# Attention and experts of a transformer layer on one core: two instruction blocks joined into one

## What is computed

```
xn  = layernorm(x)
out = x + attention(xn) + experts(xn)

attention: 16 heads of 16, each token sees the 129 tokens within 64 positions; qkv = xn @ Wqkv + bqkv,
           softmax over the band, then @ Wout + bout
experts:   logits = xn @ router_w + router_b, the best 2 of 8 experts, softmax over these two;
           each expert is relu(xn @ w1 + b1) @ w2 + b2 with 1024 hidden numbers
```

## Time and profile before

| | us |
|---|---|
| median of 3 executions | 956.04 |
| the profiled execution | 957.17 |
| its span, from the first to the last instruction | 955.1 |
| barrier between norm_project and attend | about 100 |
| barrier between attend and experts | about 498 |
| mean granted clock of TensorE, share of full | 0.988 |

### The profile page before, as it was taken

The page is one execution under the profiler, slowest core; times in us unless marked ns, Lnnn a source line. Parts: engine busy times, 40 slices in busy tenths (PEclk is TensorE's granted clock), DMA queues, the critical chain, the costliest instruction groups (busy, mean ns, idle before and its releaser), DMA issues. The chain is left out here.

```text
span 955.1 us, 27555 instructions
## 1 busy us (share of the span) xinstructions
PE 903.1 (95%) x7684; PEld 876.4 (92%) x7684; DVE 824.7 (86%) x2171; ACT 740.7 (78%) x1985; POOL 480.5 (50%) x700
## 2 busy tenths in 40 slices
PE   4989799899999999999969999999999999999996
PEld 3878788889999999999969999999999999999996
DVE  5876699998888888888857999999999999999995
ACT  3545699899999999999956777777777776777773
POOL 5120013236465646555544666556666666556663
PEclk9999799999999999999998999999999999999999
DMA  4979532344444444455335222222222222221210
GB/s 143 322 268 308 169 79 75 117 122 136 136 136 135 137 135 133 136 141 148 105 87 163 37 34 44 46 36 36 34 34 43 47 49 49 35 44 35 36 22 1
DMA packets 69867, 95.33 MB, mean 100 GB/s; under 512 B 15549, under 2 KB 48960, under 8 KB 69696
## 3 DMA queue, kind: packets, MB, share of 16 engines
q1 hardware_dynamic: 52800, 77.97, 27.0%
q0 software_dynamic: 17024, 16.88, 11.2%
HBM read 62.91 MB, written 35.53 MB: 103 GB/s over the span
## 5 line engine op out<-in xcount | busy, mean ns | idle before, releaser
L1029 ACT ACTIVATE weights_qkv<-weights_qkv,low 128x256 f32<-128x256 f32 (+1 forms) x512 | 240.2, 480 | 1.1 <-DVE low L832 1.1
L1456 ACT ACTIVATE hid<-ps_experts,b_s 128x256 f32<-128x256 f32 x312 | 131.0, 473 | 117.5 <-PE ps_experts L1523 87.4
L1344 POOL DMA_INDIRECT out<-y,target x78 | 137.3, 1761 | 127.4 <-DVE y L1422 113.8
L843 DVE TENSOR_TENSOR pt<-ps_attend,pt 128x512 fp32r<-128x512 f32 (+1 forms) x256 | 158.4, 620 | 39.9 <-ACT pt L1042 39.3
L1123 PE MATMUL ps_attend<-pt,v_m 128*80 128x256 f32 (+7 forms) x1536 | 187.8, 271 | 2.3 <-DVE inv_t L856 1.8
L1539 PE MATMUL ps_experts<-w_hi,h_hi 128*128 128x256 f32 x624 | 175.4, 281 | 1.1 <-DVE h_lo L1391 1.1
L1523 PE MATMUL ps_experts<-xgt_hi,w_hi 128*128 128x256 f32 x624 | 173.7, 278 | 2.8 <-DVE xgt_lo L1382 2.8
L1123 PEld LDWEIGHTS ps_attend<-pt,v_m 128*80 128x80 f32 (+3 forms) x1536 | 171.4, 162 | 4.2 <-issue 4.2
L1523 PE MATMUL ps_experts<-xgt_hi,w_lo 128*128 128x256 f32 x624 | 173.6, 278 | 0.0
L1523 PE MATMUL ps_experts<-xgt_lo,w_hi 128*128 128x256 f32 x624 | 173.5, 278 | 0.0
L1539 PE MATMUL ps_experts<-w_lo,h_hi 128*128 128x256 f32 x624 | 172.6, 277 | 0.0
(11 more groups left out here) (174 smaller groups left out, 2008.6 us busy)
## 6 DMA issues: line engine op xcount, KB each, us to landing
weights_qkv<-in_w SPq DMA_DIRECT2D x15, 1024.0 KB, 7.1
qk_hi<-weights_qkv SPq DMA_DIRECT2D x16, 512.0 KB, 4.8
qk_lo<-weights_qkv SPq DMA_DIRECT2D x16, 512.0 KB, 5.5
q_st<-qk_hi SPq DMA_DIRECT2D x128, 64.0 KB
k_st<-qk_hi SPq DMA_DIRECT2D x128, 64.0 KB
weights_qkv<-in_x SPq DMA_DIRECT2D x8, 512.0 KB, 4.3
xn_rows<-weights_qkv SPq DMA_DIRECT2D x8, 512.0 KB, 5.2
k_st<-qk_lo SPq DMA_DIRECT2D x64, 64.0 KB
```

Of the source, the lines that this page charges most:

```text
L843: v.tensor_tensor(lo[:, f:l], ps[:, bank_t[h], 0:l - f], hi[:, f:l].bitcast(F32), ALU.subtract).then_inc(s_plo, 1)
L1029: ins = act.activation(wt[:, ring, at_tile(i)], wt[:, ring, at_tile(i)], ACT.Exp, bias=low[:, ring, i:i + 1], scale=-1.0, accum_out=total[ ...
L1344: pool.indirect_dma_start(out_tokens, bass.IndirectOffsetOnAxis(ap=target[:, h:h + 1], axis=0), y[:, h], None, bounds_check=T - 1, oob_is_ ...
L1456: ins = act.activation(hid[:, n % 2, j], ps[:, bank_h[n], j * ROWS:(j + 1) * ROWS], ACT.Relu, bias=b1[:, ds(e * FC + 2 * n + j, 1)])
```

## The change

Attention and experts become one block; the block of norm_project stays. `g.block` is opened once, and both functions add their instructions to it, so each engine goes from its last instruction of attend to its first of experts with no barrier. For that:

- The operands of the experts become views of buffers that attention has finished with: `w1_hi`, `w1_lo` and the rows of ring 1 lie in `q_st`, `w2_hi` in `v_m`, `w2_lo` in `k_st`, `xt_hi`, `xt_lo`, the rows of ring 2 and `h_hi` in `work` (which is `pt` during attention), `h_lo` in `split` (which is `a_hi` and `a_lo`). The same two buffers hold `xt_lo`, `w_lo` and `xt_hi` of norm_project.
- The 65 semaphores of both stages are raised once, by GpSimd in norm_project, and so are the two `s_out`.
- GpSimd fetches the rows of step 0 (`gather_first`) within the last batch, after the bias additions of head 14 and ahead of head 15.
- The preamble of the experts moves into the tail of attend, between its instructions.
- `ident_r` is copied in norm_project and `b1` is loaded in the first batch of attend.

```diff
@@ norm_project, GpSimd; below it VectorE
+                start(pool, g.later.values())
+                start(pool, g.s_out)
                 pool.wait_ge(s_rstd, 1 + START)
                 pool.memset(g.q_st[:].bitcast(F32), 0.0).then_inc(s_zero, 1)
...
+                v.wait_ge(s_ident, 2 + START)
+                v.tensor_copy(g.ident_r[:], g.ident[:])
                 statistics(0, 0)
@@ attend, SyncE
                 def first_batch():
                     next_stack(0, 2)
+                    sp.dma_start(g.b1[:], g.b1_cols).then_inc(s_b1, 16)
                     next_stack(0, 3)
...
-                sp.wait_ge(s_rows, 16 + START)
-                sp.wait_ge(s_wload, 32 * (E - 1) + 16 + START)
@@ attend, GpSimd, in the loop over heads
                             if last:
                                 add_bias(b, 1, n - 14)
+                        if last and n == 14:
+                            gather_first()
@@ attend, VectorE, behind the last batch
+                first = v.value_load(g.step_expert[0:1, 0:1], min_val=0, max_val=E - 1)
...
+                lo_of_w1(0)
                 v.wait_ge(s_pv, HC * 2 * B + START)
                 v.wait_ge(s_invs, 2 * B + START)
...
-                add_projected(B - 1, 0, bank_t[0])
-                add_projected(B - 1, 1, bank_t[1])
+                v.wait_ge(s_xhi, 1 + START)
+                v.tensor_tensor(g.xt_lo..., ps[:, bank_t[0], :], g.xt_hi..., ALU.subtract).then_inc(s_xlo, 1)
+                for h in range(2):
+                    add_projected(B - 1, h, bank_last[h])
+                lo_of_w1(1)
+                half = slice(0, FC // 2)
+                v.wait_ge(s_w2hi, 1 + START)
+                v.tensor_tensor(g.w2_lo[:, half], g.w2_of(first)[:, half], g.w2_hi[:, half].bitcast(F32),
+                                ALU.subtract).then_inc(s_w2lo, 1)
@@ attend, ScalarE, behind the last batch
+                first = act.value_load(g.step_expert[0:1, 0:1], min_val=0, max_val=E - 1)
...
+                act.wait_ge(s_wlast, 16 + START)
+                hi_of_w1(0)
                 inverse_out(2 * B - 1, False)
+                hi_of_w1(1)
                 act.wait_ge(s_proj, 2 * (B - 1) + START)
                 for h in range(2):
                     act.wait_ge(s_enda, h + 1 + START)
                     act.activation(a_hi[:, 1, half_of(h)], ...).then_inc(s_endhi, 1)
+                act.wait_ge(s_tr4, 1 + START)
+                act.activation(g.xt_hi..., ps[:, bank_t[0], :], ACT.Copy).then_inc(s_xhi, 1)
+                act.wait_ge(s_wload, 32 * (E - 1) + START)
+                act.activation(g.w2_hi[:, half], g.w2_of(first)[:, half], ACT.Copy).then_inc(s_w2hi, 1)
@@ attend, TensorE, behind the last batch
                 transpose_inverse(2 * B - 1)
                 weighted_values(B - 1, heads - 1)
+                for h in range(2):
+                    project(B - 1, h, range(0, 6), bank_last[h])
+                for h in range(2):
+                    pe.wait_ge(g.s_g[h], 16)
                 for c in range(DC):
                     for h in range(2):
-                        project(B - 1, h, range(6 * c, 6 * c + 6), bank_t[h])
+                        ins = pe.transpose(ps[:, bank_t[0], ...], g.gathered[0][:, h, c * P:(c + 1) * P], g.ident_r[:])
+                ins.then_inc(s_tr4, 1)
+                for h in range(2):
+                    project(B - 1, h, range(6, 12), bank_last[h])
@@ experts, GpSimd
                 for n in range(1, RING):
+                    if n == 1:
+                        pool.wait_ge(s_s, DC * HC * B + START)
+                    else:
+                        pool.wait_ge(s_pv, DC * HC * B + START)
+                    pool.memset(g.gathered[n].bitcast(F32), 0.0).then_inc(s_xz, 1)
...
                     gather(n, n, n)
@@ build
-            attend(nc, g)
-        experts(nc, g)
+        with nc.Block() as g.block:
+            attend(nc, g)
+            experts(nc, g)
```

More of the change, by code:

```diff
@@ L3 @@
 import math
-from contextlib import ExitStack
+from contextlib import ExitStack, nullcontext
 import concourse.bass as bass
@@ L506, in sb, with sem @@
             return ctx.enter_context(nc.sbuf_tensor(name, shape, dt))
[L508 to L513, removed]
+        def sem(name):
+            return g.later[name]
         W = 2 * P
@@ new lines, in attend @@
+        s_bias = sem("s_bias")
+        s_bo = sem("s_bo")
+        s_top = sem("s_top")
+        s_pick = sem("s_pick")
+        s_gap = sem("s_gap")
+        s_ratio = sem("s_ratio")
+        s_count = sem("s_count")
+        s_rank = sem("s_rank")
+        s_placed = sem("s_placed")
+        s_vm = sem("s_vm")
+        s_s = sem("s_s")
+        s_low = sem("s_low")
+        s_exp = sem("s_exp3")
+        s_t = sem("s_t")
+        s_phi = sem("s_phi")
+        s_plo = sem("s_plo")
+        s_pv = sem("s_pv")
@@ new lines, in attend @@
+        s_rec = sem("s_rec")
+        s_invt = sem("s_invt")
+        s_inv = sem("s_inv")
+        s_invs = sem("s_invs")
+        s_a = sem("s_a")
+        s_ahi = sem("s_ahi")
+        s_alo = sem("s_alo")
+        s_proj = sem("s_proj")
+        s_proj0 = sem("s_proj0")
+        s_done = sem("s_done")
+        s_biased = [sem("s_biased0"), sem("s_biased1")]
+        s_entry = sem("s_entry")
+        s_rows = sem("s_rows")
+        s_idx = sem("s_idx")
+        s_named = sem("s_named")
+        s_wlast = sem("s_wlast")
@@ L1365, in _ @@
             def _(v):
-                start(v, by["v"])
                 def lo_of_w1(s, e, n):
@@ L1431, in _ @@
             def _(act):
-                start(act, by["act"])
                 def hi_of_w1(e, n):
@@ L1591, in build @@
         g.first_rows = sb("first_rows", [P, 2, D], F32R)
-        g.first_index = sb("first_index", [P, 2], U32)
+        g.index = sb("index", [P, RING, 2], U32)
+        g.ident_r = sb("ident_r", [P, P], F32R)
+        g.b1 = sb("b1_s", [P, E * FC])
+        g.later = {name: ctx.enter_context(nc.semaphore(name)) for name in LATER}
         g.s_g = [ctx.enter_context(nc.semaphore(f"s_g{h}")) for h in range(2)]
```

261 lines of the change are left out of this document (118 added, 143 removed).

## The result

The forecast was 945.0 us with a range of 941 to 950.5, and 95% for faster. The changed kernel takes **965.36 us** (median of 4 runs, 964.8 to 966.76) against 955.9 before on the same chip: ratio 1.0104, interval [1.0088, 1.012]. It is slower by 1.0%, clear of the noise, with a time outside the range.

What follows compares the result with a forecast made beforehand. The prediction took TensorE's unbroken expert matmuls as the bound, reached late through a barrier and a slowed clock. Gains of 9.95 + 1.1 = 11.05 us off 956.04 gave 945.0 us, range 941 to 950.5.

Steps and rivals of the forecast that it cites:

- What costs nothing: Part listing changes taken as free: GpSimd's 67 semaphore raises, ident_r, b1, row fetches, and views changing addresses, not shapes.
- the sum: Total forecast gain from the two seams, 9.95 + 1.1 = 11.05 us, taking the median to 945.0 us.
- The last part of the text: Signs of right or wrong; an attention batch of another length would mean that the buffers' places matter.
- The experts are one unbroken row of matmuls: Experts, 512 to 935 us: TensorE always busy, so reaching the first matmul earlier moves the end by as much.
- Seam of attend and experts: Passage from attention to experts without the barrier: 9.95 us gained, 3.06 of it clock, the rest gap.
- rival 1: TensorE's clock falls at the new attend-experts seam too: price 5.1 us, 950.1 us; chance 11%.
- Rival 3: GpSimd is held behind its fetch at the attend-experts seam: 955.5 us, or 957.6 for the full hold; chance 6%.
- The rule weighed there: Attend-experts seam: VectorE two-SBUF-input operations and GpSimd SBUF reads exclude each other; VectorE's w1 low part up to 1.3 us later.
- Seam of norm_project and attend: Barrier stays, but TensorE's eight semaphore raises behind it go: first score earlier, 1.1 us gained; clock fall taken as unchanged.
- rival 2: The clock is kept at the first seam, norm_project to attend: gain 3 us more, 942.0 us; chance 19%.

Runs made afterwards that it cites:

- e8: The kernel before with a 192-byte gap ahead of xgt_hi, putting both operands of every expert matmul at offset 192 modulo 256: 977.64 us, ratio 1.0235.
- e6: The changed kernel with 64 unused bytes ahead of work, the q_st rows view 64 bytes further, and ident_r ahead of index: 943.92 us, ratio 0.9875.
- e11: e6 with eight semaphore raises on TensorE ahead of attention's first score: 944.78 us.
- e1: Separate kernel, TensorE alone: groups of 48 expert-type matmuls at 49 pairs of operand starts; only two groups reached 5.61 and 5.62 us.
- e5: Separate kernel, TensorE alone: sixteen rows of eight matmul groups, varying operand starts and starting moment; 113.3 to 120.0 ns a matmul.
- e12: e6 with weights at offset 64 instead of 192 and tokens still at 0, by gaps ahead of q_st and work: 952.01 us, ratio 0.9968.
- e2: The changed kernel with 64 unused bytes ahead of work, so weights at offset 192 and tokens at 0: 953.97 us, ratio 0.9979.
- e9: e6 with attend and experts each in its own block again, so the barrier between them is back: 951.5 us, ratio 0.9954.
- e10: e6 with GpSimd fetching the experts' first rows behind head 15 instead of ahead of it: 947.22 us.

## Why the prediction was wrong

- **The step that failed** is in "What costs nothing": "The views change addresses, not shapes." It took the price of an address for nothing and looked no further; the trace of before can't show that price, but the diff shows that the operands of all 3744 expert matmuls move. By the prediction's own rule (bounds where the trace shows nothing) it should have stood in the sum. What the runs show in its place: with equal start offsets a matmul took 0.1200 us and not 0.1133, which cost 22.4 us in the experts, twice the whole gain; e8 costs the kernel before 22.3 us by its offsets alone, and e6 takes the loss away by the offsets alone. The last part of the text named buffers' places as what might show in the length of an attention batch; that was the wrong place: between head 0 of batch 6 and of batch 7 it is 46.5 us after and 46.6 before. The right place was the expert step, where the two operands moved against each other (192 and 0 became 192 and 192) and nothing but TensorE sets the pace.
- "The experts are one unbroken row of matmuls [...] nothing behind it can swallow the gain" is true of waits. It also means that nothing hides a slower matmul: the same row passes on up to 0.0067 us (0.1200 - 0.1133) 3744 times.
- **Seam of attend and experts**, 9.95 us: right. Measured from head 15's transposes the effective start went from 506.05 - 486.88 = 19.17 us to 8.97, in e6 to 493.35 - 484.38 = 8.97 too: 10.2. GpSimd's fetch takes 3.48 us (481.76 to 485.24) for 3.47; L1132, now L1183, stands 3.62 us behind head 15 and not 2.11, late by 1.51 for 1.70; the clock stays up (1.00 from 488 to 512 us), so rival 1 did not happen. Rival 3 (GpSimd held behind its fetch) did not happen either: the fetch ends at 485.24, the v columns start at 485.24 and the inverse at 485.63.
- The rule weighed there shows, but the other way round: GpSimd waited, not VectorE. The last two bias additions take 2.42 us beside VectorE's L1030, which takes 1.53; without each other the additions took 1.43 (head 14's, at 480.39) and L1030 1.21 (its second, at 492.53). By that rule of the Trainium skill (SBUF — State Buffer, section "SBUF: two separate sides") the trace agrees. TensorE waited for neither.
- **Seam of norm_project and attend**, 1.1 us: right within what can be told (idle 1.21 shorter, 0.9 by e11). The clock still falls there in e6 (mean 0.62 over the stretch that had 0.50); in the profiled run of the changed kernel it fell for a shorter time (mean 0.84), so rival 2 came true in part. Of the 2.8 us by which attention is further ahead at head 15 than at its first score, 1.7 fall in its first batch, where the clock dips, 0.4 in its second and some 0.1 in each later one. This is why the 14.4 us above are 10.2 + 1.4 + 2.8.
- **The sum**: a gain of 11.05 us against 11.4 in e6 (943.92 after 955.33), where the expert matmuls have their pace of before. The terms were right in kind and size; one was missing. That they agree to 0.4 us is in part luck: in e6's trace the first score is 2.2 us earlier, not 1.1, and five groups run at the second pace.

What stays open is the mechanism. TensorE loads the next stationary operand while the moving one streams (weight loads and matmuls are both busy for 423.00 of 423.00 us), and a pace that depends on the difference of the two addresses, that locks in a few matmuls and stays, looks like two periodic readers of SBUF that fall into step. That is argued; no run showed the reads. The Trainium skill (TensorE: Matmul & The Clock Gate, section "Step-by-step: what each phase is for") says that the two operands come through independent read ports, so that loading the next weights "doesn't steal SBUF read bandwidth from the running matmul". No run here shows the ports. What the runs do show for these F32R matmuls of 128 x 256 is that a stream of them takes 0.1133 to 0.1200 us each by where the two operands start relative to each other, and by the moment, so the two are not independent in their effect on the pace. Whether other types or widths do the same wasn't tried, nor why an identity at another offset shifts the start of layer 2 just so.

## What to carry to other kernels

Where TensorE is the bound and both operands change from matmul to matmul, a change that only moves buffers can be a change of the inner loop (shown here for one type and one shape): compare the start addresses of the two operands modulo 256 bytes before and after, and count matmuls in a fixed stretch, since the busy share stays at 100% either way. Price what the trace can't show, and above all what is multiplied by thousands; a few microseconds at a seam are won once. If a version comes out slower all over, try a gap of 64 bytes before giving up the idea: here it and 32 bytes for an identity turned +1.0% into -1.3%.

## What the runs showed of the hardware that I had not expected

- The spacing of F32R matmuls of 128 x 256 is 0.1200 us with equal starts modulo 256 bytes (0.1182 in one pair of e1) and with the moving operand 96 bytes further, and from 0.1133 to 0.1200 at other differences. Only with the stationary operand 64 bytes past the moving one did groups settle at 0.1133 by themselves, and not at every moment of the start (9 of 16 in e5, 39 of 39 in e12).
- The pace is held through a group at constant addresses, and can be handed on to the next group: e2 ran two steps of six at one pace and four at the other to the end. Twice it changed where one matmul had come some 0.01 to 0.02 us late (e6, e9).
- GpSimd's drain at the end of a block with indirect DMAs ended 5.4 to 5.5 us beyond its last operation, behind a fetch or behind plain additions, and 3.6 at the end of the kernel; in a block without them, 0.1.
- A wait of 4.08 us at a barrier cost TensorE 2.7 us more, nearly all by the clock (e9), and one of 2.76 us among short work brought the clock down as well (e10: mean 0.66 from 494 to 497 us); the 1.36 us for the inverse in e6 did not (1.00 from 488 to 512 us).
